# Value products of a windowed attention spread over two column halves of the PE array, 36 columns each

## Chip, cores and metric

The program runs on one core of a Trainium2 chip. The time is the device time of one execution in microseconds, from the first to the last instruction; of several runs the median stands for a kernel. The engines are named as in the profile: PE is TensorE (PEld its weight loads), DVE is VectorE, ACT is ScalarE, POOL is GpSimd, SP issues nearly all DMAs.

## The reference

One layer: pre-norm attention and a pre-norm mixture of experts, each added to its input, on x of 2 x 1024 x 128 in fp32. The attention has 16 heads of 8. Each block of 64 queries looks at a band of 64 keys in its own and the previous block, and at four levels of pooled keys (8 a level), whose exponentials count 8, 16, 32 and 64 fold in numerator and denominator.

```python
S = einsum('bcqd,bckd->bcqk', Qc, Kwin)          # 64 queries x 128 keys a block; a band of 64 counts
As = [S[band]] + [einsum(q, Kprev[l]) for l in 1..4]
mn = min over the levels of max(A)
exps = [exp(A - mn) for A in As]
esum = exps[0].sum(-1) + sum(scale[l] * exps[l].sum(-1))
out = (exps[0] @ Vwin + sum(scale[l] * exps[l] @ Vprev[l])) / esum
x = x + out @ W_proj + b_proj
x = x + sum over 8 experts of gate[e] * ((a_e * sigmoid(b_e)) @ Wo + bo)   # a_e, b_e from W1[e]; top 2
```

## The kernel before

The attention is worked off in eight units: unit u is batch u // 4 and a group of four heads, u % 4. A unit has 16 blocks of 64 queries. Its scores come in ten slots: slots 0 and 1 hold the scores against the pooled keys (8 products each, L1172), slots 2 to 9 the scores of two blocks each against their 128 keys for four heads (2 products, L1179). ACT takes the exponential of each slot out of one of three score banks (L732, L737), DVE zeroes what is outside the band (L978), and PE forms the value products.

The value products are transposed: the stationary operand is a table of values, the moving one the exponentials of 64 queries. Per block, four products (one a head, L1198) take the table `vaug` [128 keys, 64 columns]: columns 0 to 31 are four heads of 8 value columns, of which only the eight of the product's own head are filled, and columns 32 to 63 hold ones in the eight columns of that head, so that their rows of the result are the denominator, eight times over. A fifth (L1199) adds the pooled part from `vpool`, likewise 64 columns, whose last 32 hold the weights (filled from a constant of 32 columns at C_DEN). The result of a block is 64 partitions x 64 queries in PSUM. These are fp32 products; PE runs each as two passes, a weight load before each. A step ("out", u, k) is two blocks, so 10 products or 20 passes, and there are 64 steps.

Eight blocks, half a unit, fill partitions 0 to 63 of one bank, and halves take turns between banks 3 and 4. A step ("norm", u, h) then moves half a unit out of PSUM with two ACT instructions: partitions 0 to 31 to `attT` (L748) and 32 to 63 to `denom` (L749), 32 x 512 each. Once a batch, SP sends the denominators to a compact tile `dcomp` (L497, one DMA that takes every eighth partition), DVE takes the reciprocals, SP sends them back (L501), a product spreads them over the value rows (L1108), and DVE multiplies and adds the projection.

The order on all engines is one list, SCHEDULE, written by schedule() (L132 on); each engine walks it and does its own part of each step. A step ("out", u, k) stands three slots behind its scores. A "norm" is put into the list behind the second out step (k % 4 == 1) after its half is complete; POOL reads the same step as the sign to copy the values of the half after next (values_of, L574 on). Each unit needs first: stacked queries, keys and pooled keys of its heads, sent by SP in DMAs within SBUF (L434; 3 for qst, 3 for pks, 3 for kst, 4 for qmk), the pooled keys spread by head on ACT ("heads", L410, four a unit), and the shift: an estimate of the scores' maximum from the "guard" products (L1100), reduced on DVE, transposed (L1104) and sent by SP into the stacks in two DMAs (load_shift), which the first pooled score of the unit waits for. SP takes its DMAs in program order: for unit 4 these are the denominators of batch 0, the stacks of unit 6, the reciprocals, the keys and head queries of unit 5, and then the shift of unit 5.

After the attention come the experts: 128 steps ("hidden", t, e) of three products of 512 columns (L1045 to L1047) into five banks in turn (two of them banks 3 and 4), a sigmoid on ACT (L759), a product with the gate on DVE (L1028), a sum on POOL (L654).

Of the kernel before, what the change touches and what calls it, by code (L numbers as in the profile page):

```python
# [53 lines left out]
HR = GH * DH  # L54
SR = SLOTS * HR
# [12 lines left out]
C_IOTA = C_DEN + GH * DH  # L68
# [8 lines left out]
def shape_constants(np):  # L77
# [10 lines left out]
    for j in range(GH):  # L88
        c[j * LK:(j + 1) * LK, C_DEN + j * DH:C_DEN + (j + 1) * DH] = weight[:LK, None]
# [46 lines left out]
def schedule():  # L136
# [9 lines left out]
    def attend():  # L146

        u, k = local.pop(0)
        s.append(("out", u, k))
        if k % 4 == 1 and norms:  # L150
            s.append(norms.pop(0))
        if k % 4 == 3:
            norms.append(("norm", u, k // 4))
# [7 lines left out]
        4: {0: [("v", 1, 1)], 2: [("norm", 3, 1)], 5: [("rden", 0)], 8: [("spread", 0, 0)],  # L161
# [70 lines left out]
def build(nc, x_d, wattn_d, battn_d, wproj_d, bproj_d, wg_d, w1_d, b1_d, wo_d, bo_d, const_d, out_d):  # L232
    ctx = ExitStack()
    with ctx:
# [45 lines left out]
        vpool = sb("vpool", [P, NB, NG, WIN])  # L280
# [5 lines left out]
        vaug = [sb(f"vaug{i}", [P, NB // 2, GH, WIN]) for i in range(2)]  # L286
# [133 lines left out]
        def _(sp):  # L420
# [73 lines left out]
            def load_denominators(b):  # L494

                sp.wait_ge(norm_done, 2 * NG * (b + 1))
                sp.dma_start(dcomp[:, :], denom[0:P:DH, :]).then_inc(den_in, 16)  # L497
# [49 lines left out]
        def _(gp):  # L547
# [56 lines left out]
            for i in range(2):  # L604
                then(gp.memset(vaug[i][:, :, :, :], 0.0))
                for j in range(GH):
                    ins = gp.memset(vaug[i][:, :, j, 32 + j * DH:32 + (j + 1) * DH], 1.0)
# [18 lines left out]
            for step in SCHEDULE:  # L626
                if step[0] == "norm":
# [30 lines left out]
        def _(act):  # L658
# [10 lines left out]
            for step in SCHEDULE:  # L669
# [71 lines left out]
                elif kind == "norm":  # L741

                    _, u, h = step
                    hu, rows, cols = 2 * u + h, slice(32 * (u % NG), 32 * (u % NG + 1)), slice(512 * h, 512 * (h + 1))
                    act.wait_ge(out_done, 4 * (hu + 1))
                    if u == NG and h == 0:
                        wait_gen_full(act, ("proj", 0, 1))
                    act.activation(attT[rows, cols], bank[3 + hu % 2][0:32, :], ACT.Copy)  # L748
                    act.activation(denom[rows, cols], bank[3 + hu % 2][32:64, :], ACT.Copy).then_inc(norm_done, 1)  # L749
# [21 lines left out]
        def _(dve):  # L771
# [66 lines left out]
            def weight_columns():  # L838

                then(dve.tensor_copy(vpool[:, :, :, 32:64].rearrange("p c g d -> p (c g) d"),  # L840
                                     const[:, C_DEN:C_DEN + 32].unsqueeze(1).broadcast_to([P, NB * NG, 32])))
# [35 lines left out]
            dve.memset(vpool[:, :, :, 0:32].rearrange("p c g d -> p (c g) d"), 0.0)  # L877
            then(dve.memset(xpool[:, :, :, :], 0.0))
            hn = lo = 0
            for step in SCHEDULE:  # L880
# [101 lines left out]
                elif kind == "rden":  # L982
                    dve.wait_ge(den_in, 16 * (step[1] + 1))
                    dve.reciprocal(dcomp[:, :], dcomp[:, :]).then_inc(rden_ready, 1)
                elif kind == "spread":
                    _, b, h = step
                    cols = slice(512 * h, 512 * (h + 1))
                    dve.wait_ge(norm_done, 2 * NG * (b + 1))
# [255 lines left out]
```

## Time and profile before

| | us |
|---|---|
| median of 3 runs | 335.55 |
| lowest, highest | 331.0, 336.18 |
| span of the profiled execution | 336.2 (the run of 336.18) |
| PE busy | 305.9 (91%) |
| PEld, DVE, ACT, POOL busy | 260.7, 226.8, 178.1, 142.3 |
| attention, first to last value product | 55.3 to 221.8 |
| experts | 222.0 to the end |

A timeline row gives a group's start, the time from its start to the end of its last instruction, and how many instructions it merges. The end of a matmul is modelled, and matmuls are pipelined: what one costs is read from the distance between starts. "PEclk" is the granted clock as a share of 2.4 GHz; 0.5 is 1.2 GHz.

### The profile page before, as it was taken

The page shows a single profiled execution, that of the slowest core. Times are in us where ns is not written, and L with a number is a line of the kernel's source. Part 1 is how long each engine was busy: PE and PEld are TensorE (multiplying, and loading weights), DVE is VectorE, ACT ScalarE, POOL GpSimd, SP SyncE. Part 2 cuts the span into 40 slices and gives each one's busy share as a digit, 9 for nine tenths or more (in the row PEclk, how much of TensorE's full clock was granted, in tenths as well). Part 3 has the DMA queues.
Part 4 walks back from the last instruction along what each step waited for, and adds up shares of the span by engine and source line. Part 5 has one row for each costly group of instructions (what it writes and reads, how often), then busy time and mean ns, then how long its engine had stood idle before and what let it go on. Part 6 is the DMA issues. An engine that isn't in the chain of part 4 may idle for free.

```text
span 336.2 us, 6934 instructions
## 1 busy us (share of the span) xinstructions
PE 305.9 (91%) x2384; PEld 260.7 (78%) x2384; DVE 226.8 (67%) x660; ACT 178.1 (53%) x366; POOL 142.3 (42%) x232
## 2 busy tenths in 40 slices
PE   0268699899999999999999999999999999999995
PEld 0246589788988989887989899886888867888884
DVE  6997408987585550285666655947786798777773
ACT  1513166557546842654576654574548655555552
POOL 3990011330012100010050665208778847888882
PEclk9997555999999997589999979999999999999999
DMA  7005405252304500033526013000000000000000
GB/s 225 27 1 121 104 18 117 57 118 59 96 11 94 127 18 10 1 89 101 118 64 179 11 50 108 4 10 8 8 10 18 11 0 16 11 16 8 11 17 17
DMA packets 15881, 17.51 MB, mean 52 GB/s; under 512 B 2235, under 2 KB 12646, under 8 KB 15846
## 3 DMA queue, kind: packets, MB, share of 16 engines
q1 hardware_dynamic: 15648, 16.85, 19.4%
q8 instruction: 19, 0.31, 0.4%
q10 hardware_dynamic: 198, 0.22, 0.3%
q14 instruction: 16, 0.13, 0.1%
HBM read 4.21 MB, written 1.05 MB: 16 GB/s over the span
## 4 chain that ended last, share of the span: by engine, by line
PE 76%; DVE 14%; issue 4%; ACT 3%; POOL 1%; DMA 1%; ACTq 0%; DVEq 0%
PE bank L1198 16%; PE bank L1045 12%; PE bank L1047 11%; PE bank L1046 11%; PE bank L1172 5%; PE bank L1179 4%; PE bank L1199 4%; PE bank L1100 2%; PE bank L1159 2%; PE bank L1087 2%; DVE xnorm L802 2%; DVE lmax L954 2%; PE bank L1122 2%; DVE work L978 1%; DMA xres<-L_attn_x 1%
## 5 line engine op out<-in xcount | busy, mean ns | idle before, releaser
L654 POOL TENSOR_TENSOR work<-work 128x256 f32<-128x256 f32 x110 | 80.9, 739 | 33.6 <-DVE work L1028 21.0
L1198 PE MATMUL bank<-work,vaug 128*64 128x64 f32 x1024 | 84.1, 231 | 0.3 <-issue 0.3
L1198 PEld LDWEIGHTS bank<-work,vaug 128*64 128x64 f32 x1024 | 72.8, 143 | 8.9 <-issue 1.2
L1028 DVE SCALAR_TENSOR_TENSOR work<-bank,comb,work 128x256 f32<-128x256 f32 x128 | 59.1, 480 | 25.7 <-ACT work L759 24.4
L759 ACT ACTIVATE work<-bank 128x256 f32<-128x256 f32 x128 | 48.4, 385 | 44.7 <-PE bank L1047 44.5
L978 DVE TENSOR_TENSOR work<-work,const 128x512 f32<-128x512 f32 x64 | 46.2, 734 | 18.0 <-ACT work L737 17.4
L586 POOL COPY vaug<-vwin 128x64 f32<-128x64 f32 x64 | 16.1, 298 | 94.8 <-ACT vwin L697 48.0
L737 ACT ACTIVATE work<-bank 128x512 f32<-128x512 f32 x64 | 37.5, 594 | 27.2 <-PE bank L1179 26.8
L1199 PE MATMUL bank<-work,vpool 128*64 128x64 f32 x256 | 36.9, 227 | 0.0
L562 POOL TENSOR_TENSOR rstd<-veps,nhalf 128x4 f32<-128x4 f32 x8 | 11.5, 1432 | 49.6 <-DVE veps L794 49.5
L1179 PE MATMUL bank<-qmk,kst 98*128 98x256 f32 x128 | 31.0, 328 | 0.0
L1045 PE MATMUL bank<-qmk,xT_hi 128*128 128x512 f32 x64 | 27.4, 428 | 0.1
L1045 PE MATMUL bank<-qmk,kst 128*128 128x512 f32 x64 | 26.5, 414 | 0.0
L1199 PEld LDWEIGHTS bank<-work,vpool 128*64 128x64 f32 x256 | 26.2, 143 | 0.0
L1047 PE MATMUL bank<-qmk,xT_lo 128*128 128x512 f32 x64 | 25.3, 395 | 0.0
L1046 PE MATMUL bank<-arena,xT_hi 128*128 128x512 f32 x64 | 25.3, 395 | 0.0
L1047 PE MATMUL bank<-qmk,kst 128*128 128x512 f32 x64 | 25.1, 392 | 0.0
L1046 PE MATMUL bank<-arena,kst 128*128 128x512 f32 x64 | 25.0, 391 | 0.0
L410 ACT ACTIVATE pkm<-pks,const 96x512 fp32r<-96x512 f32 x30 | 20.8, 712 | 5.5 <-DMA pks<-kpool_hi 5.5
L1179 PEld LDWEIGHTS bank<-qmk,kst 98*128 98x128 f32 x128 | 21.6, 209 | 2.4 <-issue 0.8
L954 DVE TENSOR_REDUCE lmax<-bank 128x12 f32<-128x96 f32 x64 | 13.5, 252 | 13.1 <-PE bank L1100 12.6
L1172 PE MATMUL bank<-qst,pkm 104*128 104x64 f32 x128 | 20.0, 309 | 0.0
(194 smaller groups left out, 534.6 us busy)
## 6 DMA issues: line engine op xcount, KB each, us to landing
qst<-arena SPq DMA_DIRECT2D x24, 128.0 KB, 2.3
kst<-arena SPq DMA_DIRECT2D x24, 128.0 KB, 2.3
qmk<-qst SPq DMA_DIRECT2D x32, 96.0 KB
pks<-kpool_hi SPq DMA_DIRECT2D x16, 64.0 KB, 2.0
xnorm<-L_ffn_W SPq DMA_DIRECT2D x4, 256.0 KB, 2.9
out<-yout SPq DMA_DIRECT2D x16, 64.0 KB, 1.5
xres<-L_attn_x SPq DMA_DIRECT2D x2, 256.0 KB, 4.2
xres<-L_attn_x SPq DMA_DIRECT2D x1, 512.0 KB, 7.3
```

The source lines that it names most:

```text
L654: gp.tensor_tensor(gacc[t % 2][:, :], gacc[t % 2][:, :], gtmp[(adds - 1) % TMP_RING][:, :], ALU.add).then_inc(acc_done, 1)
L737: act.activation(prob[lo % P_RING][:, :, :, :], bank[sc % SCORE_BANKS][:, :].rearrange("p (c j q) -> p c j q", c=2, j=GH), ACT.Exp).then_i ...
L759: act.activation(sig[hn % SIG_RING][:, :], bank[hn % HID_BANKS][:, HID:2 * HID], ACT.Sigmoid).then_inc(sig_done, 1)
L978: dve.tensor_tensor(prob[lo % P_RING][:, :, :, :].rearrange("p c j q -> p (c j) q"), prob[lo % P_RING][:, :, :, :].rearrange("p c j q -> p ...
L1028: dve.scalar_tensor_tensor(dst[:, :], bank[hn % HID_BANKS][:, 0:HID], comb[:, t, e:e + 1], sig[hn % SIG_RING][:, :], ALU.mult, ALU.mult).t ...
L1045: pe.matmul(out, lhs[0], rhs[0], start=start, stop=False)
L1046: pe.matmul(out, lhs[0], rhs[1], start=False, stop=False)
L1047: return pe.matmul(out, lhs[1], rhs[0], start=False, stop=stop)
L1172: ins = pe.matmul(out[:, k * WIN:(k + 1) * WIN], pkm[s][0:SR + 2 * GH, c, :, :].rearrange("p j k -> p (j k)"), qst[s][0:SR + 2 * GH, c * W ...
L1179: ins = pe.matmul(out[:, k * 256:(k + 1) * 256], kst[s][0:SR + 2, c * WIN:c * WIN + P], qmk[s][0:SR + 2, :, c * WIN:(c + 1) * WIN], start= ...
L1198: pe.matmul(o, vaug[hu % 2][:, c % 8, j, :], prob[lo % P_RING][:, i, j, :], start=(j == 0), stop=False)
L1199: ins = pe.matmul(o, vpool[:, c, u % NG, :], probp[u % 2][:, c, :], start=False, stop=True)
```

## The change

The table of a value product gets 36 columns: 32 value columns, and one denominator column a head in place of eight. A block's result then goes either to partitions 0 to 35 (even blocks) or 64 to 99 (odd blocks) of the bank, that is to the lower or the upper 64 columns of the array. In a step the products of the two blocks take turns, head by head. Step k of a unit writes columns 64k to 64k+63 of one bank, so that a unit fills one bank, and units, not halves, take turns between banks 3 and 4. The products, 10 a step, are as many as before.

"norm" is one step a unit: four ACT instructions, two for the even and two for the odd blocks, 32 x 512 to `attT` and 4 x 512 to `denom`, written to every other block of 64 columns. It stands behind step k = 1 of the next unit. The sign for POOL is now a step of its own, ("values", u, h), where the norm of a half stood. The denominators of a batch lie in 4 x 4 partitions, and four DMAs take them to `dcomp`. The memsets and constants of the denominator columns get narrower.

```diff
+VC = HR + GH
-C_IOTA = C_DEN + GH * DH
+C_IOTA = C_DEN + GH
...
@@ schedule(), attend() @@
-        if k % 4 == 1 and norms:
-            s.append(norms.pop(0))
+        if k % 4 == 1:
+            s.extend(norms)
+            norms.clear()
         if k % 4 == 3:
-            norms.append(("norm", u, k // 4))
+            norms.append(("values", u, k // 4))
+        if k == NB // 2 - 1:
+            norms.append(("norm", u))
...
-        4: {0: [("v", 1, 1)], 2: [("norm", 3, 1)], 5: [("rden", 0)], 8: [("spread", 0, 0)],
+        4: {0: [("v", 1, 1)], 2: [("norm", NG - 1)], 5: [("rden", 0)], 8: [("spread", 0, 0)],
...
-        vpool = sb("vpool", [P, NB, NG, WIN])
+        vpool = sb("vpool", [P, NB, NG, VC])
...
-        vaug = [sb(f"vaug{i}", [P, NB // 2, GH, WIN]) for i in range(2)]
+        vaug = [sb(f"vaug{i}", [P, NB // 2, GH, VC]) for i in range(2)]
...
@@ sync: load_denominators(b) @@
-                sp.wait_ge(norm_done, 2 * NG * (b + 1))
-                sp.dma_start(dcomp[:, :], denom[0:P:DH, :]).then_inc(den_in, 16)
+                sp.wait_ge(norm_done, NG * (b + 1))
+                for g in range(NG):
+                    sp.dma_start(dcomp[g * HR:(g + 1) * HR, :], denom[g * HR:g * HR + GH, :]).then_inc(den_in, 16)
...
@@ scalar: "norm" @@
-                    _, u, h = step
-                    hu, rows, cols = 2 * u + h, slice(32 * (u % NG), 32 * (u % NG + 1)), slice(512 * h, 512 * (h + 1))
-                    act.wait_ge(out_done, 4 * (hu + 1))
-                    if u == NG and h == 0:
+                    u = step[1]
+                    ob, g = bank[3 + u % 2], u % NG
+                    act.wait_ge(out_done, 8 * (u + 1))
+                    if u == NG:
                         wait_gen_full(act, ("proj", 0, 1))
-                    act.activation(attT[rows, cols], bank[3 + hu % 2][0:32, :], ACT.Copy)
-                    act.activation(denom[rows, cols], bank[3 + hu % 2][32:64, :], ACT.Copy).then_inc(norm_done, 1)
+                    by_parity = [x[:, :].rearrange("p (k e q) -> p k e q", e=2, q=WIN) for x in (attT, denom)]
+                    for e in range(2):
+                        blocks = ob[:, :].rearrange("p (k q) -> p k q", q=WIN)
+                        act.activation(by_parity[0][g * HR:(g + 1) * HR, :, e, :], blocks[64 * e:64 * e + HR], ACT.Copy)
+                        ins = act.activation(by_parity[1][g * HR:g * HR + GH, :, e, :], blocks[64 * e + HR:64 * e + VC], ACT.Copy)
+                    ins.then_inc(norm_done, 1)
...
@@ tensor: "out" @@
-                    ob = bank[3 + hu % 2]
+                    ob = bank[3 + u % 2]
                     pe.wait_ge(mask_done, lo + 1)
                     if k % 4 == 0:
                         pe.wait_ge(vaug_ready, hu + 1)
-                        if hu >= 2:
-                            pe.wait_ge(norm_done, hu - 1)
+                    if k == 0 and u >= 2:
+                        pe.wait_ge(norm_done, u - 1)
...
-                    for i in range(2):
-                        c = 2 * k + i
-                        o = ob[0:64, (c % 8) * WIN:(c % 8 + 1) * WIN]
-                        for j in range(GH):
-                            pe.matmul(o, vaug[hu % 2][:, c % 8, j, :], prob[lo % P_RING][:, i, j, :], start=(j == 0), stop=False)
-                        ins = pe.matmul(o, vpool[:, c, u % NG, :], probp[u % 2][:, c, :], start=False, stop=True)
+                    o = [ob[64 * e:64 * e + VC, k * WIN:(k + 1) * WIN] for e in range(2)]
+                    for j in range(GH):
+                        for e in range(2):
+                            pe.matmul(o[e], vaug[hu % 2][:, (2 * k + e) % 8, j, :], prob[lo % P_RING][:, e, j, :], start=(j == 0), stop=False)
+                    for e in range(2):
+                        c = 2 * k + e
+                        ins = pe.matmul(o[e], vpool[:, c, u % NG, :], probp[u % 2][:, c, :], start=False, stop=True)
```

On PE, the first local slot of unit 1 with the value products of unit 0's second half (`vaug1` is that half's table; L1100 and L1109 are guard products of unit 2, L1179 and L1188 local scores). Before:

```order
L1100 MATMUL bank6<-pkm0,qst0 128x256
L1179 MATMUL bank0<-qmk1,kst1 128x256 [waits qmk_in1,kst_in1,exp_done]
L1179 MATMUL bank0<-qmk1,kst1 128x256
L1198 MATMUL bank4<-work,vaug1 64x64 [waits mask_done]
L1198 MATMUL bank4<-work,vaug1 64x64 x3
L1199 MATMUL bank4<-work,vpool 64x64
L1198 MATMUL bank4<-work,vaug1 64x64 x4
L1199 MATMUL bank4<-work,vpool 64x64
```

After:

```order
L1109 MATMUL bank6<-pkm0,qst0 128x256
L1188 MATMUL bank0<-qmk1,kst1 128x256 [waits qmk_in1,kst_in1,exp_done]
L1188 MATMUL bank0<-qmk1,kst1 128x256
L1206 MATMUL bank3<-work,vaug1 36x64 [waits mask_done]
L1206 MATMUL bank3<-work,vaug1 36x64 x7
L1209 MATMUL bank3<-work,vpool 36x64 x2
```

The eight products of the heads now stand together, then the two pooled ones; the number and the wait are the same, the shape is 36x64 for 64x64.

On ACT, the stretch over the start of unit 1 (L732 and L737 are exponentials of pooled and local scores, L676 belongs to the next batch, L410 spreads pooled keys by head, L748 and L749 move results out of PSUM). Before:

```order
L732 ACTIVATE work<-bank2 128x512 [waits score_full]
L737 ACTIVATE work<-bank0 128x512 [waits out_done,score_full]
L748 ACTIVATE attT<-bank3 32x512 [waits out_done]
L749 ACTIVATE denom<-bank3 32x512
...
L676 ACTIVATE xT_hi<-bank5 128x512 [waits gen_full]
L737 ACTIVATE work<-bank1 128x512 [waits out_done,score_full]
L748 ACTIVATE attT<-bank4 32x512 [waits out_done]
L749 ACTIVATE denom<-bank4 32x512
L410 ACTIVATE pkm1<-pks,const 96x16x32 [waits score_full,pks_in]
L737 ACTIVATE work<-bank2 128x512 [waits out_done,score_full]
```

After:

```order
L681 ACTIVATE xT_hi<-bank5 128x512 [waits gen_full]
L742 ACTIVATE work<-bank1 128x512 [waits out_done,score_full]
L756 ACTIVATE attT<-bank3 32x8x64 [waits out_done]
L757 ACTIVATE denom<-bank3 4x8x64
L756 ACTIVATE attT<-bank3 32x8x64
L757 ACTIVATE denom<-bank3 4x8x64
L414 ACTIVATE pkm1<-pks,const 96x16x32 [waits score_full,pks_in]
L742 ACTIVATE work<-bank2 128x512 [waits out_done,score_full]
```

The pair of the first half has moved four slots back, behind it the head columns and the next exponentials.

On SP, after the shift of unit 4. Before:

```order
L434 DMA qmk<-nshiftT 2x32x128 [waits gen_dve]
L434 DMA qst<-nshiftT 8x8x128
L497 DMA dcomp<-denom 128x1x128 [waits norm_done]
L434 DMA qst<-arena 32x1024 [waits qmk_in0,score_full,gen_dve]
```

After:

```order
L438 DMA qmk<-nshiftT 2x32x128 [waits gen_dve]
L438 DMA qst<-nshiftT 8x8x128
L502 DMA dcomp<-denom 32x1x128 [waits norm_done]
L502 DMA dcomp<-denom 32x1x128 x3
L438 DMA qst<-arena 32x1024 [waits qmk_in0,score_full,gen_dve]
```

Three more issues stand before the stacks of unit 6 and all that follows them.

## Rows read from the trace of the kernel before

**Rows 1.** Page, part 1, and the granted clock over 40 slices of the span
```profile
PE 305.9 (91%) x2384; PEld 260.7 (78%) x2384; DVE 226.8 (67%) x660; ACT 178.1 (53%) x366; POOL 142.3 (42%) x232
...
PEclk9997555999999997589999979999999999999999
```
**Rows 2.** Page, part 5: value products and their weight loads; busy, mean ns
```profile
L1198 PE MATMUL bank<-work,vaug 128*64 128x64 f32 x1024 | 84.1, 231 | 0.3 <-issue 0.3
L1198 PEld LDWEIGHTS bank<-work,vaug 128*64 128x64 f32 x1024 | 72.8, 143 | 8.9 <-issue 1.2
...
L1199 PE MATMUL bank<-work,vpool 128*64 128x64 f32 x256 | 36.9, 227 | 0.0
```
**Rows 3.** Timeline of PE at full clock: start, us, instructions
```profile
119.21 0.63 PE L1198 MATMUL bank<-work,vaug 128*64 128x64 f32 x8
119.68 0.28 PE L1199 MATMUL bank<-work,vpool 128*64 128x64 f32 x2
```
**Rows 4.** Busy time by stretch, unit 5: PE, PEld, DVE, ACT, POOL, clock, DMA
```profile
159.20:176.50 17.30, 16.77 (x204) 15.09 (x202) 11.36 (x39) 11.07 (x22) 5.03 (x13) 1.00 0.36 89
```
**Rows 5.** Timeline of PE, pooled scores of unit 3
```profile
105.00 0.28 PE L1199 MATMUL bank<-work,vpool 128*64 128x64 f32 x2
105.21 1.97 PE L1172 MATMUL bank<-qst,pkm 104*128 104x64 f32 x16
107.02 0.48 PE L1179 MATMUL bank<-qmk,kst 98*128 98x256 f32 x2
```
**Rows 6.** Spreading of the reciprocals: group by form, and timeline
```profile
L1108 PE MATMUL bank<-denom,const 16*128 16x512 f32 x8 | 4.2, 627 | 0.0
...
231.47 1.98 PE L1108 MATMUL bank<-denom,const 16*128 16x512 f32 x4
```
**Rows 7.** Groups on ACT: exponentials and head columns
```profile
L737 ACT ACTIVATE work<-bank 128x512 f32<-128x512 f32 x64 | 37.5, 594 | 27.2 <-PE bank L1179 26.8
...
L410 ACT ACTIVATE pkm<-pks,const 96x512 fp32r<-96x512 f32 x30 | 20.8, 712 | 5.5 <-DMA pks<-kpool_hi 5.5
```
**Rows 8.** Timeline of SP, unit 4 to 5; PE's first pooled score; us to landing
```profile
144.84 0.61 SPq L497 DMA_DIRECT2D dcomp<-denom  x1
145.56 1.85 SPq L434 DMA_DIRECT2D qst<-arena  x3
...
155.69 0.67 SPq L434 DMA_DIRECT2D qst<-nshiftT  x1
...
159.24 1.95 PE L1172 MATMUL bank<-qst,pkm 104*128 104x64 f32 x16
...
qst<-arena SPq DMA_DIRECT2D x24, 128.0 KB, 2.3
```
**Rows 9.** Timeline of SP and PE, unit 5 to 6
```profile
161.26 1.84 SPq L434 DMA_DIRECT2D qst<-arena  x3
172.02 0.68 SPq L434 DMA_DIRECT2D qst<-nshiftT  x1
...
176.53 1.08 PE L1172 MATMUL bank<-qst,pkm 104*128 104x64 f32 x8
```
**Rows 10.** Timeline, end of the attention and start of the experts
```profile
222.74 0.59 ACT L749 ACTIVATE denom<-bank 32x512 f32<-32x512 f32 x1
...
223.35 1.28 ACT L759 ACT_TABLE_LOAD   x1
...
225.67 0.50 PE L1045 MATMUL bank<-qmk,xT_hi 128*128 128x512 f32 x1
```
**Rows 11.** Low clock: timeline of PE, then two stretches of 8 us
```profile
126.69 1.06 PE L1198 MATMUL bank<-work,vaug 128*64 128x64 f32 x8
127.54 0.42 PE L1199 MATMUL bank<-work,vpool 128*64 128x64 f32 x2
...
136.00:144.00 8.00, 8.00 (x32) 7.06 (x32) 1.18 (x4) 4.77 (x10) 1.48 (x8) 0.50 0.00 1
192.00:200.00 8.00, 7.82 (x66) 7.10 (x65) 4.44 (x9) 4.53 (x10) 6.33 (x12) 0.84 0.13 35
```

More of the change, by code:

```diff
@@ L88, in shape_constants @@
     for j in range(GH):
-        c[j * LK:(j + 1) * LK, C_DEN + j * DH:C_DEN + (j + 1) * DH] = weight[:LK, None]
+        c[j * LK:(j + 1) * LK, C_DEN + j] = weight[:LK]
     c[:, C_IOTA:C_IOTA + E] = np.arange(E)
@@ L606, in _ @@
                 for j in range(GH):
-                    ins = gp.memset(vaug[i][:, :, j, 32 + j * DH:32 + (j + 1) * DH], 1.0)
+                    ins = gp.memset(vaug[i][:, :, j, HR + j:HR + j + 1], 1.0)
                 then(ins)
@@ L626, in _ @@
             for step in SCHEDULE:
-                if step[0] == "norm":
+                if step[0] == "values":
                     hu = 2 * step[1] + step[2]
@@ L838, in weight_columns @@
             def weight_columns():
-                then(dve.tensor_copy(vpool[:, :, :, 32:64].rearrange("p c g d -> p (c g) d"),
-                                     const[:, C_DEN:C_DEN + 32].unsqueeze(1).broadcast_to([P, NB * NG, 32])))
+                then(dve.tensor_copy(vpool[:, :, :, HR:VC].rearrange("p c g d -> p (c g) d"),
+                                     const[:, C_DEN:C_DEN + GH].unsqueeze(1).broadcast_to([P, NB * NG, GH])))
             def gate(b, part):
@@ L876, in _ @@
             dve.memset(xT_lo[:, 0:PAD].bitcast(F32), 0.0)
-            dve.memset(vpool[:, :, :, 0:32].rearrange("p c g d -> p (c g) d"), 0.0)
+            dve.memset(vpool[:, :, :, 0:HR].rearrange("p c g d -> p (c g) d"), 0.0)
             then(dve.memset(xpool[:, :, :, :], 0.0))
@@ L982, in _ @@
                 elif kind == "rden":
-                    dve.wait_ge(den_in, 16 * (step[1] + 1))
+                    dve.wait_ge(den_in, 16 * NG * (step[1] + 1))
                     dve.reciprocal(dcomp[:, :], dcomp[:, :]).then_inc(rden_ready, 1)
@@ L987, in _ @@
                     cols = slice(512 * h, 512 * (h + 1))
-                    dve.wait_ge(norm_done, 2 * NG * (b + 1))
+                    dve.wait_ge(norm_done, NG * (b + 1))
                     dve.tensor_tensor(attT[:, cols], attT[:, cols], bk[:, :], ALU.mult).then_inc(gen_dve, 1)
@@ L1209, in _ @@
                     elif hn == SCORE_BANKS:
-                        pe.wait_ge(norm_done, 2 * UNITS)
+                        pe.wait_ge(norm_done, UNITS)
                     if hn == 0:
```

## The prediction

> **What bounds the kernel now.** I read the page's busy shares first: TensorE is busy 91% of the span, DVE 67%, ACT 53% [rows 1]. Next the costliest groups: the value products (L1198 and L1199) are 1280 passes with 84.1 and 36.9 us busy [rows 2]. The two overlap, so I take the true cost from the timeline: eight passes start at 119.21 and the next ones at 119.68, so a pass is 0.47/8 = 58 ns, and a step of two blocks (20 passes) is 1.17 us [rows 3]. 64 such steps at 1.17 are 75 us, over a fifth of the span, all on TensorE while it is the bound: in one whole unit of the attention (159.2 to 176.5) it is busy 16.77 of 17.30 us, DVE 11.36 and ACT 11.07 [rows 4]. The tail of the kernel, the experts, has no value product in it.
>
> **What a pass waits for.** Two limits lie close together. (a) The weight load: the pooled scores load 128 weight columns for 64 streamed ones, and 16 of them take 107.02 - 105.21 = 1.81 us, 113 ns each [rows 5], which is 0.88 ns a weight column, so 64 columns want 56 ns. (b) The stream: four fp32 passes of 512 columns take 1.98 us, the last record being about 0.63 long, so (1.98 - 0.63)/3 = 0.45 us a pass [rows 6], 0.88 ns a column, and 64 columns again want 56 ns. Going to 36 value columns shortens only (a), to about 32 ns by 0.88 a column, 35 with the 2 to 3 ns that a pass has above 56. The stream of 64 stays. So the narrower weights alone gain nothing; the gain rests on the second edit, that the stream in one half of the array runs beside the stream in the other.
>
> **The change part by part.** (1) Passes. Each fp32 product is two passes in one half, then two in the other. If the halves stream side by side, two streams of 56 need 28 ns a pass, and the loads, one after another, 35: the loads bind. I take 35. Ends: 29 (loads side by side as well) and 58 (no overlap at all: the row itself); an overlap in which a load for the other half is not begun before the preceding pass of the first half has started gives, per pair, 58 + 35 = 93, or 47 a pass. At 35: 1280 x (58.4 - 35) = 30.0 us off. At 29 it is 37.6, at 47 14.6, at 58 nothing.
>
> A row speaks to the order of load and stream: a load (138 to 143 ns long in the record) and a pass come every 58 ns in one and the same half [rows 2, 3], so a load already runs beside the stream before it. The Trainium skill (TensorE: Matmul & The Clock Gate, Part 3, "What overlaps and what doesn't") says that a weight load overlaps matmuls in flight only when the row groups differ; both halves here use all 128 rows, so by it this change could not overlap its loads. By it today's pass would also cost 56 + 56 = 112 ns, and the trace has 58, so I don't follow it for the load. What is left of it is the case of 47 ns, a rival below.
>
> (2) Evictions. Per unit four ACT instructions stay four. An eviction of 32x512 is 0.59 [rows 10]; 512 elements a partition also in the new ones, so no ACT time is won from 4 in place of 32 partitions. But the two of the first half move back by four steps, so that all four (2.36 us) stand in one burst, behind which the head columns of the unit after next (0.71 each [rows 7]) and the exponentials (0.59 [rows 7]) are queued. TensorE waits for those exponentials. Its unit shrinks from 17.3 to 17.3 - 8 x 0.47 = 13.5 us while ACT keeps 11.07 and DVE 11.36 [rows 4], 82 and 84% of it. Score banks and a lag of three steps cover about two steps; I charge 0.3 us a unit, 2.5 in all (ends 0 and 8, one burst half uncovered in seven units).
>
> (3) SP's queue. The denominators of a batch go out in four DMAs for one. An issue costs SP 0.6 to 0.7: the 17 issues from 144.84 to 155.69 + 0.67 (1 for the denominators, 6 for the stacks of unit 6, 1 for the reciprocals, 7 for unit 5's keys and head queries, 2 for its shift) keep it busy without a pause to speak of, 11.52/17 = 0.68 each [rows 8]. The last two of them carry the shift of unit 5, and TensorE starts that unit at 159.24, 2.9 after their issue ends [rows 8]. Now the chain starts 1.2 later (burst of four evictions before it, where two stood) and is three issues longer (3 x 0.62 = 1.9, by the three of 1.85): 3.1 us. A transfer of this size class lands 2.3 us after its issue begins, so the shift is there at 155.69 + 2.3 = 158.0 and the slack is 1.25 (nought if it lands slower, 2.9 if at once). TensorE then starts the unit 3.1 - 1.25 = 1.85 later than today, and the 3.8 that the 8 steps before it had saved are lost as well: 5.6 us given back (ends 4 and 7). Unit 6: from the first issue after unit 5's pooled scores (161.26) to the landing of the shift (172.02 + 2.3) are 13.1 us; TensorE takes 161.0 to 176.53, 15.5 [rows 9], less 3.8 = 11.7. So 1.4 us of waiting. Unit 1, by the same reckoning, 0.5. Elsewhere SP waits for the shift, not the shift for SP.
>
> (4) End of the attention. The last eviction ends at 223.33, then ACT loads a table (1.28) and starts the sigmoids; TensorE, five banks ahead, starts its sixth product at 225.67 just as the first bank comes free [rows 10]. Two more evictions in front are 1.2 us on the path.
>
> (5) Clock. At the low level a step's eight passes take 0.85 us for 0.47 [rows 11], so whatever TensorE does in such a stretch costs as much again. The granted clock was 0.50 in 136 to 144, where projections stand and hardly a value product, and 0.84 in 192 to 200, around a unit's pooled scores; full in dense steps [rows 11, 1]. The change takes dense work out and puts waits in at just such unit starts. I charge two to three falls like that at 192 to 200 (8 x 0.16 = 1.3 us each): 4 us (ends -2 and 10). Memsets and weight columns that get narrower lie on POOL and DVE before TensorE's first use of them: nothing.
>
> The sum, against the profiled execution (span 336.2, the run of 336.18; the median of the three is 335.55, half a microsecond less): 336.2 - 30.0 + 5.6 + 1.4 + 0.5 + 1.2 + 2.5 + 4 = 321.4; against the median 320.8. I say 321.
>
> **Rivals.** A: overlap is only partial, 47 ns a pass. Passes -14.6; a unit saves 1.8 instead of 3.8, so unit 5 gives back 3.7, unit 6 nothing, tail 1.2, ACT 0.5, clock 1: 336.2 - 14.6 + 6.4 = 328.0. For it: one load for every pass, 1024 and 1024 [rows 2], and a second load ahead is nowhere seen. [...]
>
> B: no overlap; the halves share the stream. Passes 0, unit 5 +1.8, tail +1.2, clock 0 to 1: 339.2 to 340.2, no change within 2%. For it: every product streams over all 128 rows from one fetch of 64 columns. The Trainium skill (TensorEngine Tiling, "Key Properties") has tiles execute loads and matmuls in parallel, which speaks against B; no row here has two halves in use.
>
> C: slower. Going from one half to the other is paid like a change of the array's shape. Where a step ends and pooled scores begin the next pass starts at 105.21, after 105.00 and two passes (58 each): 0.21 for 0.117, 93 ns more [rows 5]. The change goes over 640 times. From 6 ns a change it costs 3.8 us and is, with B's 3.0, over 2% slower; at 93 it would be 60 us: 336.2 + 60 + 3 = 399. The same page says that only a change of the mode, not of the tile, drains the engine; both halves are one shape. A mild form (20 ns, no overlap) gives 352.
>
> D: everything overlaps (29 ns) and nothing waits but unit 5 and the tail: 336.2 - 37.6 + 6.6 (unit 5) + 2.3 (unit 6) + 1.2 = 308.7.
>
> **How the numbers follow.** Forecast (near 35 ns, 314 to 328) 0.45, D 0.08, A 0.18, B 0.20, C 0.09. Time 321. Two in ten are left out below 310 and above 340: range 310 to 340. 2% (6.7 us, about what a measurement of this kernel tells from none) is passed below 329: faster = 0.45 + 0.08 + half of A, less a little for clock falls, 0.60; same = the other half of A, B and the rest, 0.29; slower = C and B with a worse clock, 0.11.
>
> **What would show it.** Value passes (start to start) at 33 to 38 ns at full clock, a step near 0.70 us; 47 says A, 58 says B, more says C. An idle TensorE before the first pooled scores of unit 5 (4 to 6 us) released by the shift's DMA, and one of 1 to 2 at unit 6. The four evictions in one piece of 2.4 us on ACT. DVE and ACT busy over 75% of a unit. Low clock stretches at more than one unit start. The experts' part (from 222 to 336) as long as before, but for 1.2 us. I am wrong in the main thing if a step still takes 1.17, and in the terms behind it if the units 1 to 7 are each shorter by the full 3.8.

## The result, and the profile after

The changed kernel takes 344.22 us (median of 4 runs, 340.85 to 344.77); the kernel before, on the same chips, 335.87 (331.0 to 336.33). The ratio is 1.0313, with a 95% interval of 1.0214 to 1.0412: slower by 3%, where I had said 321 and faster. (Ratios here and below leave disturbed runs out, among them one of 1184 us of the kernel before at a mean clock of 0.252, so they need not be the quotient of two medians.)

The value passes did become cheap. Timeline of TensorE in the changed kernel at the full clock, then at the low one (start, us, engine, line, tiles, shapes, count):

```profile
80.69 0.64 PE L1206 MATMUL bank<-work,vaug 128*36 128x64 f32 x16
81.17 0.28 PE L1209 MATMUL bank<-work,vpool 128*36 128x64 f32 x4
81.38 0.50 PE L1188 MATMUL bank<-qmk,kst 98*128 98x256 f32 x2
```
```profile
72.78 1.08 PE L1206 MATMUL bank<-work,vaug 128*36 128x64 f32 x16
73.65 0.43 PE L1209 MATMUL bank<-work,vpool 128*36 128x64 f32 x4
74.00 0.58 PE L1109 MATMUL bank<-pkm,qst 96*128 96x256 f32 x1
```
At full clock 16 passes take 81.17 - 80.69 = 0.48 us, 30 ns each, where one half took 58 [rows 3]; all 20 of a step take about 0.6 for 1.17 (0.69 up to the next product's start, 81.38). At the low clock (the second fence; before, [rows 11]) 16 take 0.87, 54 ns each, so they gain the same factor of two there. The overlap is complete, near rival D's 29 ns rather than the 35 I took.

The time went elsewhere. Of the changed kernel, the page's busy times and its granted clock over 40 slices, beside [rows 1]:

```profile
PE 299.1 (87%) x2384; PEld 245.6 (72%) x2384; DVE 223.5 (65%) x660; ACT 177.3 (52%) x366; POOL 141.2 (41%) x232
...
PEclk9995555559698965555985856999999999999999
```
TensorE is busy for only 6.8 us less [rows 1], with some 37 us of passes gone (1280 at 29 for 58 ns), and the clock row is full of fives. The mean granted clock of the execution is 0.811, before it was 0.929. By stretch (head, attention, experts; columns as in [rows 4]: length, busy PE, PEld, DVE, ACT, POOL, clock, DMA), before:

```profile
0.00:55.30 55.30, 33.56 (x115) 26.68 (x115) 37.08 (x104) 21.73 (x34) 21.25 (x33) 0.77 0.32 84
55.30:222.10 166.80, 162.52 (x1729) 145.17 (x1728) 106.86 (x331) 94.36 (x170) 37.29 (x83) 0.93 0.27 69
222.10:336.20 114.10, 109.80 (x543) 88.88 (x542) 82.86 (x227) 62.07 (x162) 83.73 (x116) 1.00 0.04 11
```
and after:

```profile
0.00:53.70 53.70, 32.84 (x117) 26.16 (x118) 34.58 (x104) 21.71 (x34) 19.64 (x33) 0.75 0.34 86
53.70:227.40 173.70, 156.00 (x1729) 130.70 (x1728) 106.05 (x330) 92.40 (x168) 37.93 (x83) 0.70 0.27 67
227.40:342.90 115.50, 110.30 (x544) 88.70 (x542) 82.88 (x229) 63.16 (x164) 83.60 (x116) 1.00 0.04 11
```
The attention, from the first value product to the last, is 6.9 us longer, the experts with the four evictions ahead of them 1.4. (The head is 1.6 shorter in this one execution; the spans differ by 6.7, the medians by 8.35, and I can't place the rest.) Multiply length by clock to get the attention in full-speed time: 166.8 x 0.93 = 155.1 before, 173.7 x 0.70 = 121.6 after, 33.5 less. The remainder, 11.7 before and 52.1 after, is what the low level cost if everything in such a stretch took twice as long: 40.4 more. That is an upper estimate, since waits are counted in it too. The busy column gives a second one. TensorE is busy 6.5 us less (156.00 for 162.52) with 37.6 of passes gone, so its other work and what is left of the passes took 31.1 more; it idles 17.7 for 4.3 us, 13.4 more; and -37.6 + 31.1 + 13.4 = +6.9. So the change did take out about what it should. By these two estimates the low clock took back 31 to 40 us, and what idle time adds to that is at most 13.4.

The waits, one by one. TensorE's inside the attention, after (us in total, times, longest):

```profile
PE bank L1113 <- DVE nshift_parts L974: 7.1, 4, 3.8
PE bank L1206 <- DVE work L987: 3.2, 5, 1.4
PE bank L1141 <- ACT xnorm L727: 2.2, 1, 2.2
PE bank L1206 <- POOL vaug L591: 2.1, 1, 2.1
PE bank L1109 <- ACT pkm L414: 1.8, 1, 1.8
```
and before, the whole list:

```profile
PE bank L1104 <- DVE nshift_parts L965: 3.8, 6, 1.6
PE bank L1198 <- issue: 0.3, 1, 0.3
PE bank L1132 <- ACT xnorm L722: 0.2, 1, 0.2
```
TensorE idles 17.7 of 173.7 us there, before 4.3 of 166.8 (length less busy in the windows). The longest wait stands ahead of unit 5, where the shift is prepared (units are counted from 0 throughout); SP's queue, DVE and TensorE after:

```profile
142.39 2.75 SPq L502 DMA_DIRECT2D dcomp<-denom  x4
145.25 1.82 SPq L438 DMA_DIRECT2D qst<-arena  x3
```
```profile
146.95 0.95 DVE L993 RECIPROCAL dcomp<-dcomp 128x128 f32<-128x128 f32 x1 [1.69 <-DMA dcomp<-denom]
```
```profile
151.18 0.39 PE L1113 MATMUL bank<-const,nshift_parts 128*64 128x128 f32 x1 [3.75 <-DVE nshift_parts L974]
```
Four issues in place of the one of [rows 8] bring the denominators later. DVE waits 1.69 us for them, and behind the reciprocals it works without a pause until 151.03, the shift's parts (L974) last; for these TensorE waits, 3.75 us where it was 0.96 before. ACT waits 5.93 us for the stacks, which stand behind the denominators too, but only until 150.40, when DVE's last reduction for the shift (150.30) has begun: that is not this path.

### The profile page after: what moved, and what is told of

It is laid out like the page before. It is cut to its first block, busy times and chain, and to the rows that moved or that the text cites. A ratio compares the mean times of both kernels' runs of the same rounds, so it can differ in the third digit from the quotient of the medians.

```text
span 342.9 us, 6940 instructions
## 1 busy us (share of the span) xinstructions
PE 299.1 (87%) x2384; PEld 245.6 (72%) x2384; DVE 223.5 (65%) x660; ACT 177.3 (52%) x366; POOL 141.2 (41%) x232
## 4 chain that ended last, share of the span: by engine, by line
PE 67%; DVE 17%; ACT 5%; issue 5%; POOL 2%; DMA 2%; SPq 1%; ACTq 0%; DVEq 0%; POOLq 0%
PE bank L1054 11%; PE bank L1056 10%; PE bank L1055 10%; PE bank L1206 9%; PE bank L1181 6%; PE bank L1188 4%; PE bank L1109 3%; DVE work L987 2%; PE bank L1168 2%; POOL rstd L567 2%; PE bank L1209 2%; PE bank L1117 2%; PE bank L1124 2%; DVE lmax L963 1%; DVE xnorm L811 1%
## 5 line engine op out<-in xcount | busy, mean ns | idle before, releaser
L1206 PE MATMUL bank<-work,vaug 128*36 128x64 f32 x1024 | 52.9, 262 | 5.4 <-DVE work L987 3.2
L1206 PEld LDWEIGHTS bank<-work,vaug 128*36 128x36 f32 x1024 | 40.9, 139 | 16.5 <-DVE work L987 7.9
L1188 PE MATMUL bank<-qmk,kst 98*128 98x256 f32 x128 | 36.5, 377 | 0.0
L1188 PEld LDWEIGHTS bank<-qmk,kst 98*128 98x128 f32 x128 | 26.5, 255 | 3.8 <-issue 2.0
L414 ACT ACTIVATE pkm<-pks,const 96x512 fp32r<-96x512 f32 x30 | 20.8, 712 | 11.6 <-DMA pks<-kpool_hi 11.5
L1181 PE MATMUL bank<-qst,pkm 104*128 104x64 f32 x128 | 25.2, 357 | 0.1
L1181 PEld LDWEIGHTS bank<-qst,pkm 104*128 104x128 f32 x128 | 24.1, 282 | 1.4 <-issue 0.7
L1109 PE MATMUL bank<-pkm,qst 96*128 96x256 f32 x64 | 21.0, 429 | 2.5 <-ACT pkm L414 1.8
```

The costliest lines, as they stand in the source:

```text
L1109: ins = pe.matmul(bk[:, i * 256:(i + 1) * 256], qst[u % 2][0:SR, t * P:(t + 1) * P], pkm[u % 2][0:SR, 2 * t:2 * t + 2, :, :].rearrange("p ...
L1181: ins = pe.matmul(out[:, k * WIN:(k + 1) * WIN], pkm[s][0:SR + 2 * GH, c, :, :].rearrange("p j k -> p (j k)"), qst[s][0:SR + 2 * GH, c * W ...
L1188: ins = pe.matmul(out[:, k * 256:(k + 1) * 256], kst[s][0:SR + 2, c * WIN:c * WIN + P], qmk[s][0:SR + 2, :, c * WIN:(c + 1) * WIN], start= ...
L1206: pe.matmul(o[e], vaug[hu % 2][:, (2 * k + e) % 8, j, :], prob[lo % P_RING][:, e, j, :], start=(j == 0), stop=False)
```

## The experiments

Two theories. CLOCK: with half the passes, the value steps no longer keep TensorE's clock up, and what they save is paid back at the low level by everything else. WAITS: SP's three further issues and the burst of evictions leave TensorE idle. A value step is called thin where its passes take about 0.6 us at full clock, as in the changed kernel, and thick where they take about 1.2, as before. "Low" below is span x 2 x (1 - mean clock), the time spent at 1.2 in place of 2.4 GHz; it is 130 us for the changed kernel and 48 for the one before. Each run's span and clock are those of its profiled execution.

**1. The narrow columns alone.** The kernel before, in one half, with tables of 36 columns and four DMAs for the denominators:

```diff
+VC = HR + GH
-                        o = ob[0:64, (c % 8) * WIN:(c % 8 + 1) * WIN]
+                        o = ob[0:VC, (c % 8) * WIN:(c % 8 + 1) * WIN]
```


> The kernel before with tables of 36 columns and four denominator DMAs, all blocks still in the lower half, two banks and evictions by halves as before. Theory CLOCK (the halves do overlap, and the time is lost because TensorE, filled for fewer microseconds, is granted 1.2 GHz for 82 us longer): a value pass stays at 58 ns, since the stream of 64 columns sets it; the clock stays near 0.93 and the time within 1% of before, 335 to 339 (the 3 longer issues on SP cost up to 2). If the clock followed the share of the array's columns that is filled rather than the time in which something streams, the mean clock would fall below 0.88 and the time rise above 340. Theory WAITS (SP's chain and the burst of four evictions cost the time): SP's part alone would show, up to +2.

336.28 (329.08 to 345.45) against 336.22 of the kernel before, clock 0.912, low 59 us. Timeline:

```profile
151.20 0.64 PE L1200 MATMUL bank<-work,vaug 128*36 128x64 f32 x8
151.67 0.28 PE L1201 MATMUL bank<-work,vpool 128*36 128x64 f32 x2
151.78 0.39 PE L1200 MATMUL bank<-work,vaug 128*36 128x64 f32 x4
```
Ten passes take 0.58 us to the next block's start. The kernel before takes 0.63 for the same (58.24 to 58.87 in its trace), and 58 ns a pass [rows 3] where there is no pause behind the first. So the stream sets the pass. Narrow weights gain some 0.05 us a step, 3 us in all, at the first block's start; neither that nor the three more issues can be told in runs that scatter like these.

**2. The halves with 64 columns.** The changed kernel with `VC = 64`, zeros in the columns that are new.

> The changed kernel with tables of 64 columns again (the last 28 are zero), halves taking turns as in it. If weight loads go one after another at 0.88 ns a column, a pass takes 56 to 58 ns at full clock, a step 1.17 us, the clock stays near 0.9 and the time is 337 to 342 in spite of the waits. If the loads of the two halves run beside each other, a pass takes 29 ns as with 36 columns, and by theory CLOCK clock and time are those of the changed kernel (0.81 to 0.84, 341 to 345).

342.87, ratio 1.0309 (1.0059 to 1.056), clock 0.843.

```profile
103.13 0.69 PE L1207 MATMUL bank<-work,vaug 128*64 128x64 f32 x16
103.65 0.29 PE L1210 MATMUL bank<-work,vpool 128*64 128x64 f32 x4
103.86 0.50 PE L1189 MATMUL bank<-qmk,kst 98*128 98x256 f32 x2
```
103.86 - 103.13 = 0.73 for 0.69 with 36 columns (first fence above), and 16 passes in 0.52, 33 ns each for 30. Loads one after another would need 20 x 56 ns = 1.12. So the loads of the two halves run side by side too, and the width of the tables hardly matters.

**3. Every product twice.** The changed kernel; 40 passes a step in place of 20, sums and weights both doubled.

```diff
+                    for again in range(2):
                     for j in range(GH):
```


> The changed kernel with the ten products of every step issued twice (the second time writes the same results over the first), so that TensorE does 37 us more of streaming at full clock: a step takes 1.17 us, as long as before the change. Theory CLOCK: the granted clock returns to 0.90 or more, and the time is 336 to 341, below the changed kernel's 344 although TensorE does twice the value work. Theory WAITS: the clock is no cause but follows, and the added work comes on top where TensorE does not wait: 360 or more.

341.9 (334.84 to 343.12), clock 0.955, low 31 us. A little above the 336 to 341 expected, far below the 360 of WAITS. 37 us of passes were added to the changed kernel and it became no slower:

```profile
PEclk9999999999999986585999989999999999999999
```

**4. Half of the value work left out.** The kernel before, one half of the array, without the products of the odd blocks; its DMAs, waits and pairs of evictions are those of before, but an eviction reads each even block for two.

```diff
-                    for i in range(2):
+                    for i in range(1):
```


> The kernel before without the value products of the odd blocks (the even blocks' results are read in their place by the same two evictions): one half of the array, 64 columns, ten passes of 58 ns a step, so 0.59 us, as in the changed kernel, 37 us of work less; SP's queue and the evictions are as before the change. Theory CLOCK: the clock falls to 0.80 to 0.87 here too and the time is 325 to 345, so most of the 37 us is given back without any of the new waits. Theory WAITS: the clock stays near 0.9 and the time falls to 300 to 312.

346.64 (340.41 to 348.03), at or above the end of what CLOCK gave, clock 0.811, low 130 us.

```profile
PEclk9997555559679655585895765999999999999999
```
Nothing of the change is in this kernel but the thinness of its steps (ten passes of 58 ns), and it has about the changed kernel's time, clock and low time. Less work made it 10 us slower. Waits appear here by themselves too (15.7 us idle in the attention), so most of the changed kernel's 17.7 don't come from its own two edits either.

**5. That half issued twice.** The control to 4, with all else in it kept.

```diff
+                    for again in range(2):
                         for i in range(1):
```


> The kernel before without the value products of the odd blocks, as in the run that left them out (the output's odd blocks are copies of the even ones), but with the ten products that are left of a step issued twice, so that a step is again 20 passes of 58 ns in one half. All else of that run stays, its evictions that read one block for two too. CLOCK (TensorE's clock is lost where the value steps are thin): mean granted clock back from 0.81-0.87 to 0.90-0.93, the low stretches back from 130 us to 50-70, time 333-339, some 8 to 10 us less than with half the passes. EVICTIONS or anything else in that edit made the slow time: stays at 343-348 or rises by the 640 passes of 58 ns, 37 us.

335.09 (331.1 to 337.07, 10 runs) against 335.75, ratio 0.9988 (0.991 to 1.0067), clock 0.933, low 45 us. Twenty passes a step again, of which ten are repeats, and 11.5 us are won; the slowest of these ten runs (337.07) is faster than the fastest of experiment 4 (340.41). CLOCK, as expected (the low time a little below the 50 to 70); nothing else in the edit of 4 was slow.

The first unit, unit 0, shows how. Stretches from about its start on: the kernel before, the changed one, experiment 4 and experiment 5, in this order.

```profile
56.00:76.00 20.00, 17.77 (x204) 16.02 (x203) 17.86 (x65) 9.55 (x17) 6.91 (x11) 0.96 0.41 99
```
```profile
54.00:78.00 24.00, 21.84 (x206) 18.65 (x202) 18.06 (x67) 8.75 (x15) 7.34 (x11) 0.50 0.38 92
```
```profile
56.00:79.00 23.00, 20.93 (x124) 18.23 (x122) 17.64 (x64) 9.21 (x16) 6.79 (x9) 0.52 0.36 87
```
```profile
56.00:76.00 20.00, 18.26 (x205) 16.30 (x205) 17.88 (x62) 9.82 (x17) 6.83 (x11) 0.95 0.41 99
```
All four come out of the projections at the low clock. By the clock's own record in the trace, where steps are thick it is full again at 57.4 (before) and 58.1 (5); where they are thin it stays low through the unit, to 78.0 and 77.9. Waits don't tell them apart: TensorE idles 2.2, 2.2, 2.1 and 1.7 us in the four stretches. Nor do the records' busy shares, 89 to 91% whatever the clock, nor the count of matmuls alone: the changed kernel has 206 there, the kernel before 204. What differs is how long the value passes of a step take from start to start at full clock. Nor is idle time needed for a low clock. In experiment 4 it stays at 0.50 for 34 us without any, over unit 3 and the next batch's projections:

```profile
115.50:149.60 34.10, 34.10 (x168) 29.45 (x166) 12.30 (x40) 17.60 (x34) 1.48 (x8) 0.50 0.09 23
```
The Trainium skill (TensorE: Matmul & The Clock Gate, Part 1) has the gate follow how busy the engine has been lately. The busy share of these records does not bear this out; which measure the gate takes no run here tells.

The other traces agree, with a spread. The stretch inherited from the projections ends between 56.7 and 58.1 where all steps of unit 0 are thick or partly thick (before and experiments 1, 5, 6, 11 and the second kernel of 12), and between 65.1 and 78.0 where all are thin (the changed kernel and 2, 4, 8, 9, 10). With two thick steps at the unit's end it ends at 65.9 and 67.8 (7, and 8 with 7). So thin steps lengthen it by 7 to 21 us, and what sets how much is open: 2 and the changed kernel differ only in zero columns and end at 65.1 and 78.0.

**6. Part of the work repeated.** The changed kernel, two of five products per block issued once more: 28 passes a step.

```diff
+                    for j in range(2):
+                        for e in range(2):
+                            pe.matmul(o[e], vaug[hu % 2][:, (2 * k + e) % 8, j, :], prob[lo % P_RING][:, e, j, :], start=(j == 0), stop=(j == 1))
                     for j in range(GH):
```


> The changed kernel with the first four of the ten products of every step issued once more ahead of it, 28 passes for 20: a middle dose between the changed kernel (0.59 us a step) and the one that issues all twice (1.17). Theory CLOCK: the granted clock lies between theirs (0.81 and 0.95), about 0.86 to 0.93, the time 333 to 343, not above the changed kernel's 344. Theory WAITS: each step only adds its 0.23 us, 15 us in all at most: 350 to 359.

337.16 (334.53 to 342.43), ratio 1.0162 (0.9863 to 1.046), clock 0.897, low 69 us: between 20 and 40 passes in low time, and 7 us faster than the changed kernel with 15 us of passes added.

**7. Repeated beside the pooled scores only**, steps k = 4 and 5 of each unit.

```diff
+                    for again in range(2 if k in (4, 5) else 1):
```


> The changed kernel with the ten products issued twice only in the last step before and the first step behind a unit's pooled scores (16 of 64 steps, 9 us of streaming at full clock). Theory CLOCK, in its local form (the clock falls at the sparse starts of the units and then stays low): fewer low stretches, clock 0.85 to 0.92, time 332 to 341. If the clock is set by the whole of a unit and not by its start, the clock stays at 0.80 to 0.84 and the time at 342 to 350. Theory WAITS: 346 to 353.

340.37 (333.71 to 341.6), clock 0.869, low 89 us: 4 us better with 9 us of work added, in the range that CLOCK gave, though single runs scatter by as much. Thickening two steps of eight seems to help some, less than experiment 6 in all eight.

**8. Without the two new waits.** 57 columns, so that the sums of weights lie 8 apart and one DMA takes them, and evictions two and two.

```diff
-VC = HR + GH
+VC = HR + 3 * DH + 1
-                for g in range(NG):
-                    sp.dma_start(dcomp[g * HR:(g + 1) * HR, :], denom[g * HR:g * HR + GH, :]).then_inc(den_in, 16)
+                sp.dma_start(dcomp[:, :], denom[0:P:DH, :]).then_inc(den_in, 16)
-                    for e in range(2):
+                    for e in (step[2],):
```


> The changed kernel without its two new waits and with nothing added: the denominator columns lie eight apart again (57 columns a table), so one DMA takes a batch's denominators as before the change, and the four evictions of a unit are two and two, four slots apart. Theory WAITS: 336 or less, since the 5 to 9 us that I had charged come back. Theory CLOCK: the low stretches stay (clock 0.80 to 0.86), and the time is 338 to 345.

337.41 (334.46 to 341.05), ratio 1.0165 (0.9843 to 1.0487), clock 0.852, low 99 us: 6.8 better, between the two ranges given (336 or less for WAITS, 338 to 345 for CLOCK, whose clock of 0.80 to 0.86 it has). TensorE still idles 17.5 us in the attention. So the gain isn't idle time removed; the low stretches became shorter. Why they did isn't shown.

**9 and 10. The two waits one at a time.** One DMA with the burst kept, then pairs of evictions with four DMAs kept.

> The changed kernel with 57 value columns in place of 36 (the four sums of weights 8 columns apart), so that the denominators of a batch go out in one DMA as before; the burst of four evictions stays. WAIT ON SP's QUEUE: TensorE's wait before the heads of unit 5's shift (3.75 us in the changed kernel, by denominators, stacks and heads) falls by the three issues, 1.9 us, and the time by 2 to 3 to 341-342. CLOCK: shorter idle also moves where the clock falls, so anything from 338 to 344 with a clock of 0.80-0.86. NO SHARE of SP's queue: 344 as the changed kernel.

> The changed kernel with its four denominator DMAs, but the four evictions of a unit in two pairs, the second one four steps later, as they stood before the change. BURST: if the burst on ACT is what costs, 338-340, and the run with one DMA alone stays near 343; if SP's three issues are it, this one stays at 343-345. With both undone it was 337.4; the two parts should add up to that gain of some 6 to 7 us if nothing but waits is at work, and need not where the clock decides.

One DMA: 340.74 (335.78 to 344.53), low 113 us; pairs: 342.15 (339.17 to 343.23), ratio 1.0214 (1.0112 to 1.0315), low 120 us. 3.5 and 2.1 us, together 5.6 of the 6.8; single runs scatter by as much. The wait itself goes as worked out. DVE and TensorE of the first, TensorE's waits of it, and the timeline of the second:

```profile
144.10 0.95 DVE L992 RECIPROCAL dcomp<-dcomp 128x128 f32<-128x128 f32 x1
...
148.33 0.39 PE L1112 MATMUL bank<-const,nshift_parts 128*64 128x128 f32 x1 [1.88 <-DVE nshift_parts L973]
```
```profile
PE bank L1112 <- DVE nshift_parts L973: 7.3, 5, 2.1
```
```profile
146.12 0.39 PE L1118 MATMUL bank<-const,nshift_parts 128*64 128x128 f32 x1 [5.01 <-DVE nshift_parts L979]
```
Without the three issues DVE no longer waits for the denominators, and TensorE's wait ahead of unit 5 falls from 3.75 to 1.88, by 1.9 as expected, though all five waits of this kind together stay at 7.3 for 7.1. With the issues and the pairs it is 5.0. Pairs at 342.15 meet neither range given, 338 to 340 if the burst is what costs and 343 to 345 if the issues are.

**11. Both cures together**, experiments 8 and 6.

> The changed kernel without its two new waits (one denominator DMA, evictions two and two) and with four of the ten products of a step issued twice, 28 passes a step in place of 20. Each of the two alone gave 337.4 and 337.2 for 344.2 of the changed kernel. CLOCK: fewer low stretches than with either alone (below 65 us), mean clock 0.90-0.93, 331-335, at or a little below the kernel before (335.9). TENSOR-BOUND without a clock effect: 337.4 plus 64 x 8 x 29 ns = 15 us, 352.

338.58 (336.09 to 345.74), ratio 1.0101 (1.0017 to 1.0185), clock 0.883, low 79 us. A miss: neither the 331 to 335 of CLOCK nor 352. The cures don't add up: the inherited stretch ends at 57.0, but the clock falls again from 60.4 to 67.2, and six more times. 8 with 7 (expectation below) gave 337.68 (333.33 to 340.35) and clock 0.867, in the ranges of CLOCK but no better than 8 alone.

> The two before together: no new waits, and the steps on either side of the pooled scores issued twice. Theory CLOCK: clock 0.86 to 0.94 and time 326 to 338, the best of the halved kernels. If the clock does not rise over 0.85, neither place nor waits matter and only the fill of all slots does: 338 to 348.

**12. Single units.** The changed kernel with unit 0 thick, then the kernel of experiment 8 with units 0 and 4 thick.

```diff
+                    for again in range(2 if u == 0 else 1):
```
```diff
+                    for again in range(2 if u in (0, 4) else 1):
```


> The changed kernel, with the ten products of each step issued twice in the first unit alone (eight steps, 8 x 20 passes of 29 ns = 4.6 us more work). In the profile of before the low clock that the attention inherits from the projections ends at 57.4, 1.2 us after the first unit's first step; in the changed kernel it goes on to 78.0, the end of that unit. THIN STEPS HOLD THE CLOCK DOWN: with the first unit thick the low stretch ends by 57 to 61, 17 us or more earlier; the second unit's first step starts at 75 to 78 as in the changed kernel or sooner although it does 4.6 us more, and 339-345 in all, since the later stretches are left alone. INHERITED, whatever the steps hold: ends at about 78 or later, the second unit starts 5 to 9 us later, 349-353.

> The changed kernel without its two new waits, and twice the products in the two units that follow a run of projections (the first and the fifth); the other six are thin. The kernel without the two waits had 337.4 and low stretches of 99 us, the longest up to 65.4 and from 123.4 to 154.1. RECOVERY in thick steps: both of these are 8 to 15 us shorter, low clock 70-85 us, and the 2 x 4.6 us of added work are paid back: 334-339. If the other stretches (168 to 202) hold the loss, they stay and the time is 338-343.

The first: 340.16 (339.91 to 342.05), ratio 1.0289 (1.0232 to 1.0347). Its profiled execution had no low stretch in the head at all, so nothing was inherited and the question it was made for isn't answered by it. It has low 68 us, half of the changed kernel's, and is only 4 us faster with 4.6 of work added: low time is no direct measure of the loss. The second: 335.43 (335.05 to 344.63), ratio 1.0128 (1.0094 to 1.0162), low 89 us, the time as expected and the low time just above the 70 to 85; here the inherited stretch ends at 58.1, where experiment 8 alone had 65.4 and the changed kernel 78.0:

```profile
56.00:76.00 20.00, 18.03 (x367) 16.09 (x366) 18.02 (x63) 8.72 (x15) 6.93 (x11) 0.95 0.41 97
```
Nearly twice the matmuls of the changed kernel's unit 0, in four us less. From the first pooled value product of one unit to that of the next:

| us | unit 0 | 1 | 2 | 3 | 4 | 5 | 6 |
|---|---|---|---|---|---|---|---|
| before | 20.4 | 17.3 | 19.2 | 32.8 | 22.2 | 18.0 | 22.5 |
| changed | 24.0 | 17.6 | 16.8 | 29.3 | 27.7 | 21.7 | 24.1 |
| half the work (4) | 23.4 | 17.1 | 17.7 | 35.1 | 24.0 | 21.7 | 24.1 |
| that half twice (5) | 20.4 | 17.3 | 19.2 | 31.8 | 22.3 | 18.0 | 20.9 |
| experiment 8, units 0 and 4 thick | 20.2 | 19.0 | 16.0 | 29.7 | 24.6 | 21.5 | 19.0 |

In the changed kernel unit 2, mostly at full clock, is 2.4 us shorter, and unit 3 3.5, with 20 us of it at the low clock for 17 before, near the 3.8 of the forecast; units 0, 4 and 5, mostly at the low clock where before they were at full clock, are 3.6, 5.5 and 3.7 longer. No version is told from the kernel before as faster: of the ratios on record for kernels with two halves the lowest is 1.0101 (experiment 11).

## Why the prediction was wrong, point by point

- **Pass rate, step (1): right in kind, mis-sized.** I took 35 ns on the ground that loads queue one after another. They don't: 30 ns, and 33 with 64 columns (experiment 2), where one load after another would need 56. The term should have been near -37.6. The Trainium skill (TensorEngine Tiling, "Key Properties") lets different tiles load and multiply at once; the trace now agrees, with 30 ns for 58. Rivals A, B and C, all about this rate, are out.
- **Clock, step (5): the step that failed.** I charged "two to three falls", 4 us, ends -2 and 10. It cost 31 to 40 by the two estimates above. I had read "full in dense steps" [rows 11] and charged only the starts of units. The other half of that reading is that the dense steps were what lifted the clock: in before it rises at 57.4, at the end of the first value step, after 27 us at the low level (the fives of the clock row in [rows 1]). The change halves the time of just these. I had priced a fall by its own length and never asked what ends it. Experiments 4 and 5 show it as a cause: thin steps without any other edit give 346.6, the same made thick 335.1.
- **Evictions, step (2).** Four of 0.59 in one burst, as said (139.98 to 142.36 on ACT ahead of unit 5). Charged 2.5 us; undoing it gave 2.1, within the scatter of the runs.
- **SP's queue, step (3): right cause, wrong path.** I expected SP's later issues to hold up the shift's DMA and TensorE to wait for it, before unit 5's pooled scores (5.6). It waits sooner, 3.75 us ahead of the shift's own matmuls (L1113), because DVE takes the reciprocals before it reduces for the shift, and waits 1.69 for the denominators first. The four issues take 2.75 us; taking three away shortened TensorE's wait by 1.87 and the time by 3.5, which is within the scatter of the runs.
- **End, step (4): right.** 1.4 for 1.2.
- **The sum.** With the passes at 29 ns the first four steps give 336.2 - 37.6 + 5.6 + 1.4 + 0.5 + 1.2 + 2.5 = 309.8. What stands between this and 344 is mostly the clock, some 30 us. A rival "slower" was there, but on the price of changing halves; the one that came true was one of my own terms, bounded by 10 where it took 31 to 40.

What stays open: why, once the two waits are gone, partly thick steps leave 79 to 99 us low; what makes an inherited low stretch under thin steps end at 65 or at 78; and which measure the gate takes. The kernel before itself has runs near 331 us with mean clocks of 0.938 to 0.99 and runs near 336 with 0.923 to 0.978, so the mean clock alone does not rank single runs.

## What to carry to other kernels

Two column halves of the array do run two of these fp32 products at once, loads included, and halve the time of a pass. Before taking such a gain, find the places where the granted clock rises in the profile and ask whether the work that you remove or overlap is what stands there: here a saving inside it was paid back by what then ran at the low level. Compare how long that work takes there at full clock before and after (a value step 1.17 us and 0.6), since neither the busy share nor, with two products at once, the number of matmuls showed it here. Test it cheaply by leaving half of the work out: if that kernel is slower, as experiment 4 was, the saving is not on offer.

## What the runs showed that I had not expected

- Leaving out 640 passes of 58 ns, 37 us of TensorE's work, made the kernel 10 us slower (346.64 for 336.22); adding 1280 passes to the changed kernel cost nothing that the runs tell (341.9 for 344.22).
- The weight loads of the two halves overlap in full: 16 passes with 64 weight columns each in 0.52 us, 33 ns for a load that takes 56 ns in one half by my estimate from [rows 5].
- The low stretch that ended 1.2 us after the first pooled value product of a thick unit (56.2 to 57.4) went on for up to 23.5 us after that of a thin one (54.5 to 78.0), with TensorE busy about 90% of the time by its records in either. Another low stretch, in experiment 4, shows 34 us at 0.50 with no idle time of TensorE at all.
